# One attention and feed-forward layer on one core: groups of 1024 tokens in loops, or one unrolled stream of 128 slots

## What is computed

```python
w = weights[subjects]; h = einsum('bct,bcd->bdt', x, w)          # mixes the 64 tokens of a sequence
q = silu(causal_dwconv(h @ Wq, 4 taps) + b); k = likewise with Wk  # 16 heads of 128
q, k = layernorm(q) * qn_w + qn_b, layernorm(k) * kn_w + kn_b      # over the 128 of a head
v = h @ Wv; beta = sigmoid(h @ Wb + bb); gate = silu(h @ Wg)
S = (1 - b) * S + b * v k^T;  o_t = S q_t                           # scan over the 64 tokens, per head
x = x + (o * gate) @ Wo
y = x @ W2.T + lora(x)                                             # one of 8 adapters of rank 16 per sequence
xq = round(y / rms, scaled by its row's largest to 127)            # int8 grid
x = x + (xq @ ternary(ffn_w).T) * gamma * scale + bias
```

## Time and profile before

| | |
|---|---|
| median of 3 runs | 2880.14 us |
| profiled execution | 2878.08 us, of which its span 2876.0 us |
| granted PE clock, mean | 0.982 of 2.4 GHz |
| PE busy | 2600.1 us |
| VectorE, ScalarE, GpSimd busy | 1863.6, 1571.0, 1604.2 us |
| moved by DMA | 257.20 MB, 89 GB/s on average |

### The profile page before, as it was taken

How to read it: one execution, slowest core, us unless ns; L and a number is a source line. 1 busy time by engine, 2 the same in 40 slices (tenths; PEclk the granted TensorE clock), 3 DMA queues, 4 the chain that set the end, 5 groups by cost and what they waited for, 6 DMA issues and landing times.

```text
span 2876.0 us, 45128 instructions
## 1 busy us (share of the span) xinstructions
PE 2600.1 (90%) x14172; PEld 2007.4 (70%) x14184; DVE 1863.6 (65%) x2905; ACT 1571.0 (55%) x2393; POOL 1604.2 (56%) x1450
## 2 busy tenths in 40 slices
PE   4789898898999999999989999999998999999998
PEld 4657666676776777777767676767677777777766
DVE  4474856757658575666765848484765756667576
ACT  2463646547247474656535748384734746565562
POOL 2685767858626464555633727273652645556374
PEclk9999999999999999999999999999999999999999
DMA  7433324233332231222223222222233312221321
GB/s 162 154 104 97 95 85 126 80 118 98 103 113 83 66 95 59 86 75 80 86 100 102 63 85 75 72 75 71 83 101 102 95 60 86 76 80 54 106 82 44
DMA packets 207120, 257.20 MB, mean 89 GB/s; under 512 B 97370, under 2 KB 123482, under 8 KB 206938
## 3 DMA queue, kind: packets, MB, share of 16 engines
q1 hardware_dynamic: 206938, 254.49, 29.0%
HBM read 198.59 MB, written 55.84 MB: 88 GB/s over the span
## 4 chain that ended last, share of the span: by engine, by line
PE 59%; POOL 13%; issue 13%; DVE 10%; ACT 4%; SPq 1%; DMA 0%; POOLq 0%; DVEq 0%; ACTq 0%
PE pj_q L969 17%; PE m L969 10%; PE pj_k L969 9%; PE cen_q L969 5%; POOL sq_lo_k L515 4%; PE m L1113 3%; PE gen L969 3%; DVE y_k L669 3%; PE cen_k L969 3%; POOL r_odd L497 2%; PE m L1103 2%; POOL sq_lo_q L515 2%; DVE acc L720 1%; ACT y_q L890 1%; POOL og_lo L509 1%
## 5 line engine op out<-in xcount | busy, mean ns | idle before, releaser
L669 DVE SCALAR_TENSOR_TENSOR y_q<-pj_q,conv,y_q 128x504 f32<-128x504 f32 (+2 forms) x384 | 281.1, 732 | 181.3 <-ACT y_q L877 172.1
L669 DVE SCALAR_TENSOR_TENSOR y_k<-pj_k,conv,y_k 128x504 f32<-128x504 f32 (+2 forms) x384 | 281.3, 732 | 164.5 <-ACT y_k L877 155.4
L969 PE MATMUL pj_k<-ht_hi,wk 128*128 128x512 f32 x1024 | 350.2, 404 | 30.5 <-POOL wk L456 30.5
L969 PE MATMUL pj_q<-ht_hi,wq 128*128 128x512 f32 x1024 | 345.8, 399 | 17.8 <-issue 7.4
L969 PE MATMUL pj_q<-ht_hi,wg 128*128 128x512 f32 x1024 | 348.3, 401 | 0.0
L515 POOL TENSOR_TENSOR sq_lo_q<-y_q,sq_hi_q 128x512 fp32r<-128x512 f32 x128 | 191.7, 1498 | 279.5 <-ACT y_q L890 279.5
L509 POOL TENSOR_TENSOR og_lo<-gt,og_hi 128x512 fp32r<-128x512 f32 x128 | 170.1, 1329 | 174.3 <-DVE og_hi L707 174.3
L969 PEld LDWEIGHTS pj_k<-ht_hi,wk 128*128 128x128 f32 x1024 | 199.8, 195 | 79.4 <-POOL wk L456 34.0
L503 POOL TENSOR_SCALAR s_hi_q<-y_q 128x512 fp32r<-128x512 f32 x128 | 79.3, 619 | 305.2 <-ACT y_q L882 305.1
L969 PEld LDWEIGHTS pj_q<-ht_hi,wq 128*128 128x128 f32 x1024 | 195.2, 191 | 69.7 <-DVE acc L720 10.8
L969 PE MATMUL m<-wv,ht_hi 128*128 128x512 f32 x768 | 236.8, 389 | 0.0
(11 more groups left out here) (309 smaller groups left out, 6724.2 us busy)
## 6 DMA issues: line engine op xcount, KB each, us to landing
wo<-parts SPq DMA_DIRECT2D x48, 512.0 KB, 5.9
wq<-parts SPq DMA_DIRECT2D x48, 512.0 KB, 3.5
wk<-parts SPq DMA_DIRECT2D x48, 512.0 KB, 3.6
wg<-parts SPq DMA_DIRECT2D x48, 512.0 KB, 3.8
wv<-parts SPq DMA_DIRECT2D x48, 512.0 KB, 5.7
keep<-keep_rows SPq DMA_DIRECT2D x256, 64.0 KB, 2.8
parts<-wv SPq DMA_DIRECT2D x20, 512.0 KB, 3.5
parts<-wq SPq DMA_DIRECT2D x17, 512.0 KB, 3.1
```

The source lines that it names most:

```text
L669: V.scalar_tensor_tensor(out=yy[:, :, k:], in0=pp[:, :, :L - k], scalar=conv[:, i, j, 3 - k:4 - k], in1=yy[:, :, k:], op0=ALU.mult, op1=AL ...
L969: last = T.matmul(psum, a, b, start=start and n == 0 and m == 0, stop=stop and n == len(pairs) - 1 and m == 2)
```

## The change

The kernel is written anew round one stream. Groups are of 512 tokens, eight of them; with 16 heads that makes 128 units of one head on 512 tokens, and slot U of the stream starts unit U. There is no loop on any engine: 139 slots (`SLOTS = UNITS + 11`) are written out. A slot has, for PE: q and k of unit U, variance (even slots, for the two units before) or spreading of its result (odd slots), first part of the slot's tiles, scores of unit U-3, gate of U, second part of the tiles, spreading (even slots), values of U-3, centring of U. The tiles (V, output, input stage z/bt/cond, feed-forward x2/xa/h/xqt/f) are laid out by a table over the 16 slots of a group; -1 means that the tile belongs to the group before. All tiles and one of the two value halves share two PSUM banks in turn (`ring0`, `ring1`): a tile waits until the tile two before it has been taken.

```diff
-    GROUP = 1024
-    HALF = 512
+    GROUP = 512
...
-    UNITS = SET * 2
...
+    UNITS = GROUPS * H
...
+    SLOTS = UNITS + 11
...
+    5: ([("x2", -1, None, 0), ("v", 0, 1, 0), ("x2", -1, None, 1)], [("xa", -1, None, 0), ("v", 0, 1, 1)]),
...
+    7: ([("v", 0, 1, 2), ("small", -1, None, 0), ("xa", -1, None, 1)],
+        [("v", 0, 1, 3), ("quant", -1, None, 0), ("quant", -1, None, 1), ("h", -1, None, 2)]),
...
+            for U in range(SLOTS):
+                if U < UNITS:
+                    project("q", U)
+                    project("k", U)
+                if U % 2 == 0 and 2 <= U <= UNITS:
+                    variance(U // 2 - 1)
+                if U % 2 and 0 <= U - 2 < UNITS:
+                    spread(U - 2)
+                make(U, 0)
+                if 0 <= U - 3 < UNITS:
+                    score(U - 3)
+                if U < UNITS:
+                    project("g", U)
+                make(U, 1)
+                if U % 2 == 0 and 2 <= U <= UNITS:
+                    spread(U - 2)
+                if 0 <= U - 3 < UNITS:
+                    attend(U - 3)
+                if U < UNITS:
+                    centre("q", U)
+                    centre("k", U)
```

```diff
-                            T.matmul(var[x_][:], mean[:], sq_hi[x_][:], start=True, stop=False)
-                            T.matmul(var[x_][:], mean[:], sq_lo[x_][:], start=False, stop=True).then_inc(S[f"var_{x_}"], 1)
...
+                for j in range(4):
+                    mm = T.matmul(var[32 * j:32 * j + 32, :], mean[:], sq["qk"[j % 2]][:, j // 2, :], start=True, stop=True)
+                mm.then_inc(S["var"], 1)
...
+            def spread(u):
+                pe.wait_ge(S["r_split"], u // 2 + 1)
+                for i, x_ in enumerate("qk"):
...
+                    T.matmul(bc_banks[u % 2][x_][:], pick[:, 2 * (u % 2) + i, :], r_parts[:], start=True, stop=True
+                             ).then_inc(S[f"bc_{x_}"], 1)
```

```diff
+            def load_head(name, u):
+                sp.wait_ge(S[f"proj_{name}"], u)
+                if u == H:
+                    sp.wait_ge(S[f"saved_{name}"], 16 * H)
+                sp.dma_start(block_both(name, u % H), parts[name][u % H]).then_inc(S[f"w{name}_in"], 16)
```

More of the change, by code:

```diff
@@ new lines, in _ @@
+            for t in range(HT):
+                cond_lo(0, t)
+            for U in range(SLOTS):
+                if 0 <= U - 3 < UNITS:
+                    scan(U - 3)
+                if U < UNITS:
+                    taps("q", U)
+                    taps("k", U)
+                if U % 2 and 0 <= U - 2 < UNITS:
+                    normalise(U - 2)
+                if U < UNITS:
+                    silu_lo("q", U)
+                take(U, 0)
+                if U % 2 == 0 and 2 <= U <= UNITS:
+                    newton(U // 2 - 1)
+                if 0 <= U - 3 < UNITS:
+                    weigh(U - 3)
+                if U < UNITS:
+                    silu_lo("k", U)
+                if U % 2 == 0 and 2 <= U <= UNITS:
+                    split_rstd(U // 2 - 1)
+                take(U, 1)
+                if U % 2 == 0 and 2 <= U <= UNITS:
+                    normalise(U - 2)
+                if 0 <= U - 3 < UNITS:
+                    gate_out(U - 3)
@@ new lines, in take @@
+            def take(U, at):
+                for kind, n, t in tiles_at(U, at):
+                    if kind == "cond":
+                        cond_hi(n, t)
+                    elif kind == "z":
+                        beta_rows(n)
+                    elif kind == "x2":
+                        x2_high(n, t)
+                    elif kind == "h":
+                        dense_out(n, t)
+                    elif kind == "small":
+                        row_seed(n, t)
+                    elif kind == "xqt":
+                        turned(n, t)
@@ L1264, in _, with free_bank, make_cond @@
-            group(0, True)
-            with pe.Fori(1, GROUPS) as g:
-                group(g, False)
+            def free_bank(kind, n, t=0):
+                no = ring_no[kind, n, t]
+                if no > 1:
+                    pe.wait_ge(S[f"ring_free{no % 2}"], no // 2)
+            def make_cond(g, t):
+                if t == 0:
+                    pe.wait_ge(S["x_in"], 16 * (g + 1))
+                    pe.wait_ge(S["cond_in"], 16 * ROWS * (g + 1))
+                free_bank("cond", g, t)
+                for k in range(KC):
+                    mm = T.matmul(ring_bank("cond", g, t)[:, k * P:(k + 1) * P], acc[:, g % 2, t, k * P:(k + 1) * P],
+                                  cond_pair[:, t, :], start=True, stop=True)
+                mm.then_inc(made_sem("cond", g, t), 1)
@@ new lines, in dense @@
+            def dense(g, t):
+                if t == 0:
+                    pe.wait_ge(S["wo_in"], wo_loads("h", g))
+                pe.wait_ge(S["xam_lo"], 2 * g + t // 2 + 1)
+                free_bank("h", g, t)
+                cols = slice(t % 2 * P, t % 2 * P + P)
+                three(ring_bank("h", g, t)[:], [(x2_hi[:, k, cols], x2_lo[:, k, cols], w_big["o"][:, 0, k, :], w_big["o"][:, 1, k, :])
+                                                for k in range(KC)], stop=False)
+                three(ring_bank("h", g, t)[:], [(xam_hi[:, cols], xam_lo[:, cols], b_hi[:], b_lo[:])],
+                      start=False).then_inc(made_sem("h", g, t), 1)
```

1708 lines of the change are left out of this document (795 added, 913 removed), and 19 rows, old and new, of tables (SLOT_TILES, SPLIT_PARTS).

## The result

The changed kernel takes **2813.5 us** (median of 4 runs, 2812.7 to 2814.7) where the kernel before, measured beside it, took 2880.5: ratio **0.9767**, 95% interval 0.9750 to 0.9784, so 67 us or 2.3% less. The forecast was 2796 with a range of 2700 to 2890. The mechanism held and the sum is 18 us off, but that is partly luck: two of its terms are each wrong by far more, in opposite directions.

A forecast was written before the change was run, and what follows sets the result against it. The prediction took TensorE (PE) to bound the kernel. Start 61, slots 2541, stalls 84, first slots 25 and end 81 sum to 2792 us in the span, 2796 beside the median; range 2700 to 2890.

The forecast's parts named there:

- PE is what bounds it, and the new order lets it run densely: All slots: PE's 19 to 20 us cover the other engines; q projections 20.2 us apart in slots 10 to 15.
- Variance in strips, 2.4 us a pair: Variance products in even slots: records start in order, each overlapping only the next strip's first; 2.4 us a pair.
- strips overlap fully: Rival, 15%: the variance's strips are free of each other, 1.5 us less for each of 64 pairs, some 2700.
- the first nine slots: First group: a slot is bound by k's path plus a raw block's landing at about 16 us; 25 us.
- The slots' other work: PE's products per slot besides variance, such as q, k, gate 8.2, tiles 5.45, group work 1.9 us.
- The stalls of slots 5 to 9: Feed-forward chain through shared banks and VectorE's queue: some 12 us a group, seven times, 84 us.
- Order chain as the bound: Rival, 17%: thin cover in even slots and VectorE's queue set the slot; 248 us more, 3044.
- The cover of the spreading: Even slots: the split reciprocal root is ready 1 us before the spreading asks, the thinnest cover.
- Weight loads: All slots: about 2.9 MB a slot, loads land well before they are wanted; cost nothing.
- Start, 61: Before the first projection: data at 22.3 + 9.8 + 2 = 34, VectorE ends at 55, mixing tiles at 61.
- End, 81 behind slot 127's centring: After slot 127: variance to last output rows 23, output tiles 11, first transpose to end 47; 81 us.

The follow-up runs named there:

- run 2: The changed kernel with each of the four strip variance products of a pair issued a second time: 2838.4 us, ratio 0.9855.
- run 1: The changed kernel with all four variance products of a pair sent to the first strip of 32 rows: 2931.3 us, ratio 1.0181.
- Run 5: The changed kernel with four buffers in place of two for the raw weight blocks of the first 19 slots: 2752.2 us, ratio 0.9557.
- run 6: The changed kernel with another table of tiles for slots 5 to 11 (second transposes, xqt, f tiles, second row scales moved): 2770.7 us, ratio 0.9621.
- run 9: As run 6, with the third dense tile in slot 8, the second f tile behind two output tiles, V's last tile earlier: 2738.0 us, ratio 0.9498.
- Run 3: The changed kernel with the spreading of even slots ahead of the second part of the slot's tiles: 2921.8 us, ratio 1.0143.
- run 4: The changed kernel with every q, k and gate weight load's bytes copied once more, memory to memory, from slot 16: 2813.9 us, ratio 0.9769.
- run 7: The changed kernel with the first group's eight mixing loads behind the setup loads in SyncE's queue: 2813.3 us, ratio 0.9763.
- run 8: The changed kernel with the last output blocks loaded into V's free buffer and the last dense weights one set earlier: 2807.9 us, ratio 0.9743.
- run 11: The changed kernel with four raw buffers, the second table, the tail's buffers, and x and the mixing loads last at the start: 2667.2 us, ratio 0.9254.

## Why it came out so, point by point

- **PE is what bounds it, and the new order lets it run densely: right.** Slots 12 to 14 have no wait, q projections of slots 10 to 15 stand 19.0 apart on average (forecast 20.2, refuted from 21), those of slots 5 to 9 23.2 (forecast 22.5). A settled group of 327.8 is 9.6 of waits, 3.1 of low clock (what run 2 gave back in slots 5 and 8) and 315.1 of the rest, the restarts behind waits in it.
- **Variance in strips, 2.4 us a pair: wrong, it is 1.0.** This is the step that failed in the slots. The prediction read the scores' 16 records in 0.62 as records that start in order and overlap only with the next strip's first. Runs 1 and 2 show that the four strips run wholly side by side: a second round costs 0.89, one strip 2.56 more. The row that misled shows 16 records as one: their own starts in that trace lie in pairs, one for each strip, 0.01 apart, and each pair stands 0.06 behind the one before it (the second pair 0.10). So those strips ran side by side too, and of the 0.62 some 0.15 are the two ends. It is 64 x 1.4 = 90 us that the sum had too much, the rival "strips overlap fully". The Trainium skill (TensorE: Matmul & The Clock Gate, Part 3) gives 2.38x for three strips, which the prediction had set behind its own reading; carried over to four strips as it stands, 2.38 of 3 is an estimate of 1.1 us for the pair, and not the 0.9 that the prediction drew from it. The trace agrees in kind: four products of two records each go from 3.55 to 0.99. The Trainium skill (TensorEngine Tiling (Array Packing), Key Properties) also says that a change of tiling mode drains the engine. The two changes of a pair cost little here: 0.32 in place of 0.23 ahead of the first strip record, and 0.99 in place of 0.89 until the next tile, some 0.2 together.
- **Why that rival's 2700 did not come.** The rival kept the other terms, and these were short by 110. The forecast had 304 for the first group (2541 less seven times 323.2, and the 25 for its raw blocks), and it took 359.6: 56 more, although it also has seven pairs with cheap strips. The step that failed there is that of the first nine slots, k's path plus a raw block's landing at about 16 us, 25 in all. Even slots from 4 to 18, all but slot 16, took 23 to 27, because the V block's landing stands not beside k's path but inside it, in ScalarE's queue, and the reciprocal root's split behind both. Run 5 takes much of this away and the first group takes 303.5.
- **The slots' other work: close.** Without the strips' part (8 x 1.4) the forecast had 323.2 - 11.2 = 312 for 16 slots, and 315.1 are measured. Left out of the sum was, besides, the low clock behind waits, another 3.1 a group.
- **The stalls of slots 5 to 9, 12 us a group: too large (7.5, and 2.1 elsewhere), right in place for four of five.** Slot 5 waited 1.99 (2.5 forecast), slot 6 0.59 (1), slot 8 2.42 and 0.75 (2), slot 9 1.22 and 0.54 (3), slot 7 nothing (3). Runs 6 and 9 show that the table makes them: 6.6 and 11 us a group less.
- **Order chain as the bound: did not come, but only just.** The cover of the spreading, forecast as 1 us, is 1.74 in the plain even slots (the split ends at 692.93, the spreading starts at 694.67). Run 3 takes 2.7 away and is slower than before. In the first group the rival was what happened.
- **Weight loads, nothing: right** (run 4).
- **Start, 61: it was 57.75.** In the sum 22.3 + 9.8 + 2 = 34 the setup data came at 30.8. The 9.8 for the mixing loads was near (9.3); but the 22.3, read from the kernel before, held 7.4 us of issues for B2, which behind the mixing loads took 2.7 (run 7). The 27 us from the data to the first projection were right.
- **End, 81 behind slot 127's centring: 96.** The centring ends at 2715.3. To the output tiles it was 26.6 (23 forecast), for them 12.4 (11), and from the first transpose to the end 57.3 (47). The waits for weights, 4.34 and 4.54, were not in the estimate; of the 6.51 for row scales and quantising, 3.83 stood in the kernel before too, in the stretch of the earlier trace rows that it was taken from. The kernel before, then the changed one:

```profile
2865.79 0.61 PE L1233 MATMUL gen<-ident_bf,decay 128*128 128x128 bf16 x4 [3.83 <-DVE decay L810]
```

```profile
2741.90 1.22 PE L964 MATMUL ring<-wo,og_hi 128*128 128x512 f32 x2 [4.34 <-DMA wo<-parts_o]
...
2763.60 1.22 PE L964 MATMUL ring<-wo,x_hi 128*128 128x512 f32 x2 [4.54 <-DMA wo<-parts_w]
...
2802.27 0.61 PE L1076 MATMUL ring<-ident_bf,xq 128*128 128x128 bf16 x4 [6.51 <-DVE xq L649]
```

Together: 3 less at the start, 42 less in the seven later groups (78 less for 56 pairs of strips, 22 more of work, 21 more of low clock, 17 less of stalls, 10 more in slots 18 and 19, where the last four raw blocks are split), 56 more in the first, 6 less in slot 127, 15 more at the end. That is 20 above the sum's 2792, and the span is 2811.6. The forecast was near by luck: two errors met.

Left open: which of the old kernel's waits each part of the new order removed. No run puts the strips alone, or the new order alone, into the old kernel; run 1 only shows that without strips side by side the new kernel is slower than the old.

## What to carry to other kernels

Count a wait on the bound engine at more than its length: one of 0.88 cost 1.18 at full clock, since the bracket leaves out a part of the gap and the restart; and where the granted clock fell behind the waits too, 43 us of them cost 63. When one stream is laid so that its bound engine never waits, look next at its two ends and at the slots that do set-up work: there each engine's queue is read in order, and a transfer that one item waits for is a wait for everything behind it; here two more buffers were worth nearly as much as the whole rewriting. And where small products go to different strips of columns, test with one repetition what they cost, and look at the records one by one, before a pattern read from a merged row is put into a sum.

## What the runs showed of the hardware that was not expected

- **The same wait, two clocks.** Slot 5 has the same wait of 1.98 to 1.99 us for the same product in all seven groups. Behind six of them the records stand 0.43 to 0.60 apart for some 2 us (the lower level, 1.2 GHz), behind one of them 0.23 apart (the upper, 2.4 GHz), and the slot takes 23.2 or 21.7:

```profile
1191.83 1.09 PE L1052 MATMUL ring<-ident,acc 128*128 128x128 f32 x4 [1.99 <-DVE x_lo L593]
...
1194.50 0.63 PE L964 MATMUL pj_a<-ht_lo,wg 128*128 128x512 f32 x1
1194.93 0.78 PE L964 MATMUL pj_a<-ht_hi,wg 128*128 128x512 f32 x2
...
1519.60 0.63 PE L1052 MATMUL ring<-ident,acc 128*128 128x128 f32 x4 [1.98 <-DVE x_lo L593]
...
1521.11 0.39 PE L964 MATMUL pj_a<-ht_lo,wg 128*128 128x512 f32 x1
1521.34 0.63 PE L964 MATMUL pj_a<-ht_hi,wg 128*128 128x512 f32 x2
```

  In runs 1, 3, 4, 5, 7 and 8 it is again one group of the seven that has the full clock there, and not always the same one. In run 2 the strips' repetition in the even slots turned this and slot 8's low clock into the full one in all seven groups, worth 3.1 us a group. In slot 8 the wait was shorter then (1.56 for 2.42); in slot 5 it was the same 1.98. More work ahead is no rule either: run 1 puts 2.5 us more into slot 4, and slot 5 keeps its low clock in six groups. So for slot 5 the wait's length does not decide it alone; what does was not tested.
- **The same DMA issues take 2.7 to 10.9 us, by their place in the queue.** B2's four issues took 2.73 us behind the mixing loads and 10.90 when only A2's stood between them and three loads of 1 MB (run 7). They took 10.11 with two such loads ahead (run 11) and 7.36 with two ahead in the kernel before, so the number of large loads ahead does not explain it alone; what else does was not tested.
- **Four exact-F32 products in four strips** cost the time of one, 0.89 us on 512 columns, also when they are issued twice in a row.
